# Local attention stage: VectorE picks each head's own block, a projection of 8 matmuls behind the second scores, GpSimd's operands in halves

## The reference, cut to what matters

```python
def _L0_attn_ref(x, W_qkv, W_proj, b_proj, temperature):   # x: tokens, 64 channels, 8 heads of 8
    qkv = (x @ W_qkv.T).reshape(Bb, Nn, 3, NUM_HEADS, HEAD_DIM)
    ...
    attn = jnp.einsum('bhqd,bhkd->bhqk', q, k) * (scale * temperature[0])
    attn = jnp.where(mask[None, None, :, :], attn, -jnp.inf)   # |row|, |column| distance at most 3
    attn = jax.nn.softmax(attn, axis=-1)
    out = jnp.einsum('bhqk,bhkd->bhqd', attn, v)
    out = jnp.transpose(out, (0, 2, 1, 3)).reshape(Bb, Nn, C)
    return out @ W_proj.T + b_proj

h = h + _L0_attn_ref(_layernorm(h, axis=-1), ...)
```

## Time and profile before

| | us |
|---|---|
| median of 3 runs | 1732.75 |
| lowest, highest | 1726.42, 1734.28 |
| the profiled execution | 1732.1 |
| its span from first to last instruction | 1730.3 |
| TensorE busy (matmul) | 1609.0 |
| VectorE busy | 1154.8 |
| ScalarE busy | 1022.5 |
| GpSimd busy | 539.3 |

### The profile page before, as it was taken

The page is one execution under the profiler, slowest core; times in us unless marked ns, Lnnn a source line. Parts: engine busy times, 40 slices in busy tenths (PEclk is TensorE's granted clock), DMA queues, the critical chain, the costliest instruction groups (busy, mean ns, idle before and its releaser), DMA issues.

```text
span 1730.3 us, 88083 instructions
## 1 busy us (share of the span) xinstructions
PE 1609.0 (93%) x32618; PEld 1214.6 (70%) x32618; DVE 1154.8 (67%) x3381; ACT 1022.5 (59%) x2021; POOL 539.3 (31%) x699
## 2 busy tenths in 40 slices
PE   6999999779999999999996899999999999999997
PEld 4677777557888888888874666766676676667663
DVE  2566666545666666666654777787787778777762
ACT  2455555334444444444432477888888788888866
POOL 3311111055555555555542221222222122222210
PEclk9999999869999999999997899999999999999998
DMA  4201101033444444444430233333333333333322
GB/s 113 71 26 29 30 24 30 12 105 108 119 118 119 119 118 118 118 117 118 117 103 24 55 84 83 83 83 88 83 84 87 84 83 83 88 83 84 87 74 58
DMA packets 134691, 143.29 MB, mean 83 GB/s; under 512 B 42498, under 2 KB 90114, under 8 KB 134370
## 3 DMA queue, kind: packets, MB, share of 16 engines
q1 hardware_dynamic: 126306, 116.16, 25.8%
q10 hardware_dynamic: 8320, 26.22, 5.3%
HBM read 66.51 MB, written 16.99 MB: 48 GB/s over the span
## 4 chain that ended last, share of the span: by engine, by line
PE 81%; DVE 5%; issue 5%; SPq 4%; ACT 2%; DMA 1%; POOL 1%; DVEq 0%; ACTq 0%; POOLq 0%
PE ps_D L888 11%; PE ps_D L799 8%; PE ps_OT L818 4%; PE ps_J L838 4%; DVE prob L1436 4%; PE ps_D L676 3%; PE ps_AV L824 3%; SPq L463 3%; PE ps_AV L905 3%; PE ps_D L795 3%; PE ps_J L760 2%; PE ps_OT L752 2%; PE ps_J L996 2%; PE ps_J L964 2%; PE ps_OT L642 2%
## 5 line engine op out<-in xcount | busy, mean ns | idle before, releaser
L1188 ACT ACTIVATE prob<-ps_D 128x1024 bf16<-128x1024 f32 x448 | 460.3, 1031 | 123.1 <-PE ps_D L888 121.4
L1158 ACT ACTIVATE prob<-ps_D 100x512 f32<-100x512 f32 x256 | 139.0, 595 | 220.6 <-PE ps_D L799 220.6
L1351 DVE TENSOR_REDUCE m_sb<-ps_D 128x4 f32<-128x400 f32 x256 | 135.3, 570 | 89.3 <-PE ps_D L776 89.2
L799 PE MATMUL ps_D<-tile_a,key_patch 64*100 64x128 f32 x2048 | 173.8, 288 | 0.2 <-issue 0.2
L888 PE MATMUL ps_D<-tile_a,w_parts 128*128 128x256 bf16 x1024 | 155.6, 279 | 9.2 <-ACT prob L1188 1.9
L888 PE MATMUL ps_D<-tile_b,w_parts 128*128 128x256 bf16 x1024 | 151.1, 272 | 13.7 <-DVE xg L1473 4.3
L799 PEld LDWEIGHTS ps_D<-tile_a,key_patch 64*100 64x100 f32 x2048 | 135.8, 165 | 0.5 <-issue 0.4
L553 POOL TENSOR_TENSOR tile_a<-q_st,q_mask 128x1024 f32<-128x1024 f32 x64 | 123.3, 1927 | 23.0 <-PE ps_D L799 10.5
L795 PE MATMUL ps_D<-mT,key_rows 64*100 64x128 bf16 x1024 | 121.2, 227 | 8.0 <-issue 7.3
L528 POOL TENSOR_TENSOR rstd_bin<-veps_bin,minus_half 128x2 f32<-128x2 f32 x64 | 44.1, 689 | 269.9 <-DVE veps_bin L1249 269.9
L528 POOL TENSOR_TENSOR rstd_ret<-veps_ret,minus_half 128x2 f32<-128x2 f32 x64 | 46.5, 727 | 252.8 <-DVE veps_ret L1249 252.8
(11 more groups left out here) (176 smaller groups left out, 3983.2 us busy)
## 6 DMA issues: line engine op xcount, KB each, us to landing
tile_a<-xg SPq DMA_DIRECT2D x384, 64.0 KB, 2.0
tile_b<-xg SPq DMA_DIRECT2D x384, 64.0 KB, 2.0
key_st<-k_d SPq DMA_DIRECT2D x128, 162.0 KB, 3.1
tile_b<-v_d ACTq DMA_DIRECT2D x128, 120.0 KB
tile_b<-v_d ACTq DMA_DIRECT2D x64, 160.0 KB
w_exp<-experts SPq DMA_DIRECT2D x64, 129.0 KB, 2.3
xT<-in_x SPq DMA_DIRECT2D x32, 256.0 KB, 2.6
k_d<-kpad SPq DMA_DIRECT2D x64, 64.0 KB, 2.8
```

The costliest lines, as they stand in the source:

```text
L799: mm = pe.matmul(s_loc[x][0:NKL, u * P:(u + 1) * P], key_patch[rows_of(x), par, at * NKL:(at + 1) * NKL], q_block[rows_of(x), par, at * P: ...
L1158: act.activation(prob1[0:NKL, 2 * g + x, :], s_loc[x][0:NKL, :], ACT.Exp).then_inc(T2["exp_done"], 1)
L1188: act.activation(sgn[:, k % 4, :], unit(k, par)[:, :], ACT.Sign).then_inc(BN["sign"], 1)
L1351: dve.tensor_reduce(m_sb[:, C * x + HOT[x] + 4 * g:C * x + HOT[x] + 4 * g + 4], m_loc[x][:, 0:4 * NKL].rearrange("p (u n) -> p u n", u=4), ...
```

## The change

`values` signals when the sums of a strip are complete (new semaphore `sums`). `weigh` takes the reciprocal as soon as that signal has come. It then builds the one 128 x 128 block that is needed: one product and three fused product-and-add instructions, each reading one column block of ps_AV and a new 0/1 table `head_mask` (one column for each of the four lane groups), each waiting for the one before it; and a last product with the reciprocals. `project` then needs 8 matmuls with plain weights, and moves behind `scores(i, 1)`. `pre_values` moves up with that and also waits for the reciprocal of the strip before. VectorE does `pre_moments` ahead of `residual`. GpSimd makes query block and key patches of a strip in two halves of four patches each, the first half ahead of `pre_std` and released by the first scores, the second behind it; `peak` waits for its own half. SP's waits count the halves.

```diff
@@ SP, keys_in
-                sp.wait_ge(T2["q_block"], times(i - 1))
+                sp.wait_ge(T2["q_block"], times((i - 1) * 2))
...
-                sp.wait_ge(T2["k_patch"], times((i - 1) * 2))
+                sp.wait_ge(T2["k_patch"], times((i - 1) * 4))
@@ GpSimd, strip_patches(i, pair, par, part)
-                gp.wait_ge(T2["scores"], credited((i - 1) * 2))
+                gp.wait_ge(T2["scores"], credited((i - 1) * 2 - 1 + part))
-                ... q_block of 8 patches, near and far keys of 8 patches
+                ... the same of patches 4 * part to 4 * part + 3
@@ GpSimd, strip
+                if nxt:
+                    strip_patches(i + 2, j + 1, par, 0)
                 if not isinstance(m, int) or m < NS:
                     pre_std(m)
                 if nxt:
-                    strip_patches(i + 2, j + 1, par)
+                    strip_patches(i + 2, j + 1, par, 1)
@@ TensorE, peak(j, par, g)
+                pe.wait_ge(T2["q_block"], times(i * 2 + g + 1))
+                pe.wait_ge(T2["k_patch"], times(i * 4 + 2 * g + 2))
                 if g == 0:
-                    pe.wait_ge(T2["q_block"], times(i + 1))
-                    pe.wait_ge(T2["k_patch"], times((i + 1) * 2))
@@ TensorE, values: behind the sums
+                if g:
+                    mm.then_inc(T2["sums"], 1)
@@ TensorE, project
                 for t in range(2):
-                    for a4 in range(4):
-                        for r in (2 * t, 2 * t + 1):
-                            for x in range(2):
-                                at = C * (r % 2) + 32 * x
-                                mm = pe.matmul(bank["J1"][at:at + 32, t * C:(t + 1) * C], aT1[rows_of(x), a4 * P + 32 * r:a4 * P + 32 * (r + 1)],
-                                               w_p2[rows_of(x), a4, :], start=a4 == 0, stop=a4 == 3)
+                    for r in (2 * t, 2 * t + 1):
+                        for x in range(2):
+                            at = C * (r % 2) + 32 * x
+                            mm = pe.matmul(bank["J1"][at:at + 32, t * C:(t + 1) * C], aT1[rows_of(x), 32 * r:32 * (r + 1)], w_p2[rows_of(x), :], start=True, stop=True)
@@ TensorE, strip
                     pre_turn(m)
+                if m is not None:
+                    pe.wait_ge(T2["rec_done"], times(i))
+                    pre_values(m, 1 - par)
+                scores(j, par, 1)
                 if not first:
                     project(i - 1, min(i + LEAD, NS) if isinstance(i, int) else i + LEAD)
-                if m is not None:
-                    pre_values(m, 1 - par)
-                scores(j, par, 1)
@@ VectorE, weigh
+                dve.wait_ge(T2["sums"], times(i + 1))
+                dve.reciprocal(rec2[:, :], bank["OT"][:, 0:P]).then_inc(T2["rec_done"], 1)
                 dve.wait_ge(T2["av_done"], credited((i + 1) * 2))
-                dve.reciprocal(rec2[:, :], bank["OT"][:, 0:P]).then_inc(T2["rec_done"], 1)
+                dve.wait_ge(T2["proj"], times(i))
+                settle(dve)
+                for hd in range(4):
+                    src, own = bank["AV"][:, hd * P:(hd + 1) * P], head_mask[:, hd:hd + 1]
+                    if hd == 0:
+                        dve.tensor_scalar(aT1[:, 0:P], src, own, None, ALU.mult).then_inc(T2["picked"], 1)
+                    else:
+                        dve.wait_ge(T2["picked"], times(i * 4 + hd))
+                        settle(dve)
+                        dve.scalar_tensor_tensor(out=aT1[:, 0:P], in0=src, scalar=own, in1=aT1[:, 0:P], op0=ALU.mult, op1=ALU.add).then_inc(T2["picked"], 1)
                 dve.wait_ge(T2["rec_done"], times(i + 1))
-                ... one product of 128 x 512 into aT1
+                dve.wait_ge(T2["picked"], times(i * 4 + 4))
+                settle(dve)
+                dve.tensor_tensor(aT1[:, 0:P], aT1[:, 0:P], rec2[:, :], ALU.mult).then_inc(T2["attn_out"], 1)
@@ VectorE, strip
+                if more:
+                    pre_moments(nxt)
                 if not first:
                     residual(i - 1)
-                if more:
-                    pre_moments(nxt)
@@ constants: w_p2 is 128 x 64 instead of 128 x 256, head_mask (128 x 4) is one more transfer in the list of later weights
```

More of the change, by code:

```diff
@@ L80, in shape_tables @@
     t["ones_h"] = np.broadcast_to(np.arange(4)[:, None] == np.arange(32)[None, :] // HD, (P, 4, 32)).astype(np.float32)
+    t["head_mask"] = ((row % 32 // HD)[:, None] == np.arange(4)[None, :]).astype(np.float32)
     keys = np.zeros((2, C, 8, KS, KS), np.float32)
@@ L236, in build @@
         T2 = named("loc", "q_in0", "q_in1", "k_in0", "k_in1", "edge_in0", "edge_in1", "v_in0", "v_in1", "q_block", "k_patch", "max_ps", "max_done", "maxT", "negmax",
-                   "scores", "exp_done", "av_done", "rec_done", "attn_out", "proj", "h_done")
+                   "scores", "exp_done", "sums", "av_done", "rec_done", "picked", "attn_out", "proj", "h_done")
         L = named("pre", "stats", "mv", "veps", "rstd", "minus_mean", "shift", "xn", "xT_ps", "xT_sb", "kq_ps", "v_ps", "k_sb", "q_sb", "v_sb", "stored0", "stored1",
@@ L518, in _, with patches @@
             gp.wait_ge(s_prep, NLAY)
-            def patches(buf):
+            def patches(buf, part):
                 v = buf
-                near = bass.AP(v.tensor, v.offset + 8, [list(v.ap[0]), [1, 8], [NC, QP * KS]])
-                far = bass.AP(v.tensor, v.offset + 9, [list(v.ap[0]), [1, 8], [NC - 2, 2], [W, KS], [NC, 3]])
+                near = bass.AP(v.tensor, v.offset + 8 + 4 * part, [list(v.ap[0]), [1, 4], [NC, QP * KS]])
+                far = bass.AP(v.tensor, v.offset + 9 + 4 * part, [list(v.ap[0]), [1, 4], [NC - 2, 2], [W, KS], [NC, 3]])
                 return near, far
@@ L547, in bias_rows, with strip_patches @@
                                  bias2[:, :].rearrange("p (a c) -> p a c", a=1).broadcast_to((P, 2, C)), ALU.add).then_inc(L["biased"], 1)
-            def strip_patches(i, pair, par):
+            def strip_patches(i, pair, par, part):
+                own = slice(4 * part, 4 * (part + 1))
                 gp.wait_ge(T2["q_in%d" % par], times((pair + 1) * 16))
-                gp.wait_ge(T2["scores"], credited((i - 1) * 2))
+                gp.wait_ge(T2["scores"], credited((i - 1) * 2 - 1 + part))
                 settle(gp)
-                gp.tensor_tensor(q_block[:, par, :].rearrange("c (p h q) -> c p h q", h=NH, q=NQ),
-                                 q_st[:, par, :].rearrange("c (p a q) -> c p a q", a=1, q=NQ).broadcast_to((P, 8, NH, NQ)),
-                                 q_mask[:, :].rearrange("c (a h e) -> c a h e", a=1, e=1).broadcast_to((P, 8, NH, NQ)),
+                gp.tensor_tensor(q_block[:, par, :].rearrange("c (p h q) -> c p h q", h=NH, q=NQ)[:, own, :, :],
+                                 q_st[:, par, :].rearrange("c (p a q) -> c p a q", a=1, q=NQ)[:, own, :, :].broadcast_to((P, 4, NH, NQ)),
+                                 q_mask[:, :].rearrange("c (a h e) -> c a h e", a=1, e=1).broadcast_to((P, 4, NH, NQ)),
                                  ALU.mult).then_inc(T2["q_block"], 1)
@@ L558, in strip_patches @@
                 settle(gp)
-                keys = key_patch[:, par, :].rearrange("c (p n) -> c p n", p=8)
-                near, far = patches(key_st[:, par, :])
+                keys = key_patch[:, par, :].rearrange("c (p n) -> c p n", p=8)[:, own, :]
+                near, far = patches(key_st[:, par, :], part)
                 gp.tensor_copy(keys[:, :, 0:QP * KS], near).then_inc(T2["k_patch"], 1)
@@ L567, in front @@
                 gp.wait_ge(T1["scores"], times(NT))
-                strip_patches(0, 0, 0)
-                strip_patches(1, 0, 1)
+                for i in range(2):
+                    strip_patches(i, 0, i, 0)
+                    strip_patches(i, 0, i, 1)
             def strip(j, par):
@@ L817, in values @@
                             at = prob1[0:NKL, 2 * g + x, :].rearrange("k (p h r c) -> k h p r c", p=4, h=NH, r=QP)[:, 4 * e + hd, :, :, :]
-                            pe.matmul(sums[m, 4 * g:4 * g + 4, :, :], ones_h[0:NKL, hd, :], at, start=hd == 0, stop=hd == 3)
+                            mm = pe.matmul(sums[m, 4 * g:4 * g + 4, :, :], ones_h[0:NKL, hd, :], at, start=hd == 0, stop=hd == 3)
+                if g:
+                    mm.then_inc(T2["sums"], 1)
                 for u in range(4):
@@ L1502, in _ @@
             staggered(dve, strips)
-NFIRST, NLATER, NFIRST_CONST = 12, 32, 7
+NFIRST, NLATER, NFIRST_CONST = 12, 33, 7
 NSTRIP = TOK // 256
@@ L1536 @@
     arr["w_kq2"], arr["w_v2"] = np.concatenate([w[C:2 * C], w[:C]]).T, w[2 * C:].T
-    part = (np.arange(C) // HD % 4)[:, None, None] == np.arange(4)[None, :, None]
-    arr["w_p2"] = np.tile(np.where(part, n(L0_attn_W_proj).T[:, None, :], np.float32(0.0)), (2, 1, 1))
+    arr["w_p2"] = np.tile(n(L0_attn_W_proj).T, (2, 1))
     arr["b_p2"] = n(L0_attn_b_proj).reshape(1, C)
```

9 lines of the change are left out of this document (3 added, 6 removed).

## The result

| | before | changed |
|---|---|---|
| median | 1730.15 us (9 runs, 1726.42 to 1734.28) | 1738.09 us (9 runs, 1736.25 to 1740.17) |
| profiled execution | 1732.1 us, span 1730.3 | 1738.55 us, span 1736.7 |

The ratio of the times is 1.0038, 95% interval 1.0025 to 1.0051. The forecast was 1732.5 us, with a range of 1723 to 1744.

What follows compares the result with a forecast made beforehand. The prediction took TensorE's waiting for ScalarE's copy, not its work, as the limit: loop +2.5 us and stage ends -2.3 us gave +0.2 us on the profiled 1732.1. It forecast 1732.5 us, a tie, range 1723 to 1744.

Steps and rivals of the forecast that it cites:

- The hole: Ahead of pre_values, waiting for ScalarE's copy xnp: removing the projection there gains 0.06 us with par 0, TensorE idles nearly 1 us.
- rival 1: TensorE's work is the bound, as its busy share says: -45 - 12 us, 1675 us; chance 0.08.
- The stall of par 1: First peak with par 1 waits 0.43 us for GpSimd's last key copy; this goes, and pre_values loads 0.51 us earlier.
- the halves' cover: GpSimd's first half, released by earlier scores, is ready early; without that, the 0.43 us stall stays, 12 us in all.
- The projection's new place: Behind the second scores nothing hides the projection: +0.33 us a strip, from 0.26 to 0.53.
- rival 3: The projection behind the second scores reopens a 0.20 us seam: 0.53 us each, +14 us, 1744 us; chance 0.2.
- The ends: Local stage's start and written-out strips: 1.2 us gained at the turn, 0.9 us of stalls; together -2.3 us, 0 to -4.
- GpSimd: Query half 0.96 to 1.2 us, key halves 0.43 and 0.57; at most 0.8 us more a strip, costed at nothing.
- VectorE: Block's products take 1.64 us (1.0 to 2.0), block ready some 0.5 us later than before; costs nothing.
- signs written down as right: Profile after: strip period within 0.1 us of 8.58, VectorE's block finished before the next strip's copy, among others.
- Rival 2: Gap ahead of each loop turn's first scores closes, if instruction issue lags: -8 us, 1724 us; chance 0.13.
- Rival 4: VectorE's last product waits for GpSimd's query half, up to 1.1 us: +18 us, 1750 us; chance 0.06.

Runs made afterwards that it cites:

- The early copy: Changed kernel with the turn of xn ahead of the first scores and ScalarE's copy xnp ahead of the first exponentials: 1714.08 us, ratio 0.9906.
- the run with GpSimd whole: Changed kernel with GpSimd's query block and key patches whole again, behind pre_std: 1739.51 us, ratio 1.0045.
- the run with the waits moved: Changed kernel with the projection's four waits and its settle ahead of the second scores, the projection itself still behind them: 1735.18 us, ratio 1.0025.
- the run with the old place: Changed kernel with the projection of 8 matmuls back between pre_turn and pre_values: 1737.72 us, ratio 1.0045.
- the lagged version: The early copy, plus the projection of strip i - 2 behind the first peak, aT1 holding two blocks by parity: 1693.14 us, ratio 0.9787.

## Why the forecast was a tie and the time was not

**The hole: right.** 44.8 us of waits for xnp in 51 strips of the window, 0.88 us each against 0.8 to 0.9; load 0.11 us behind the copy against 0.12. The early copy, with no work taken away, gave 23 us by the ratios; rival 1, TensorE's work as the bound (1675 us), is out by 63 us.

**The stall of par 1: right in its size,** -0.51 us by the step, and what is left of the strip fits to 0.01 us. Its credit to the halves is wrong: in the run with GpSimd whole the time is the same. What ends the 0.51 us is the copy (709.98), and the projection's leaving the space ahead of pre_values is what makes them. A peak that starts late now only eats into the hole, as the 0.16 us of the run with GpSimd whole do. So the forecast that without the halves' cover 0.43 us would stay, 12 us in all, counted a stall that the hole hides; for the full 0.43 us this is an estimate, from the 1.08 us for which the loads stand idle ahead of pre_values there (at 710.93), and was not run.

**The projection's new place: the step that failed, in its size.** "I take 0.33, the row's own split" should have been 0.46. The load-to-load time was right (0.35). The step looked at the seam behind the projection and left the one ahead of it, whose 0.20 us stood in the row, to the range and to rival 3. The tell I had written down (projection to second peak, over 0.5 us) would have missed it, since it measures between loads; the stretch from scores to sums shows it. Rival 3 had the right place and the right threshold (0.45 us a strip); its price, 0.53, lacks the 0.10 us that the sums come closer to the peak. Its reason, a seam of 0.1 to 0.2 us at every switch to another shape, passed over the one switch that mattered: from the scores to the peak there was none, the load ran ahead, and the projection was put just there. The 0.13 us too little are 7.3 us over 56 strips: with them the sum is +7.5 us in place of +0.2, against +6.4 between the profiled executions and +7.9 between the medians. The loop's part of it is well founded: 28 pairs at +0.34 are 9.5 us, the mended step gives 9.8. That the whole sum comes as close is luck in part, as the next paragraph shows. (The sum gives 1732.3 on the profiled execution and 1732.95 on the medians; the 1732.5 forecast is neither, and the difference changes nothing.)

**The ends: half right.** The start: the turn of the maxima comes 6.62 us after the first peak was asked for (the fifth pre_keys), before 8.04: -1.4, where -1.2 was counted. The written-out strips did not gain the 0.9 us of stalls, nor anything else. From the first scores to the last residual the stage grew by 11.4 us, of which 28 pairs of the loop are 9.5; the eight strips lost 1.9. Stalls like that of the earlier trace rows do not follow the count of matmuls. In the last six strips those of 0.25 us and more, inside a run of like matmuls, add up to 4.2 us before and 6.5 after (the longest 1.28, 1.24, 1.46 and 1.71), but to 2.1 us in the run with the waits moved, whose work is the same. So the ends made +0.5 us (-1.4 and +1.9), where -2.3 was forecast. The rest of the span is 3.6 us shorter besides; 2.5 of that is stage one ending earlier. That varies more between executions: the local stage's first turn, behind a stage one that is the same code in all, comes between 337.99 and 345.58 us in the eleven profiles. This part of the agreement is chance.

**GpSimd: right.** Query half 1.055 us (0.96 to 1.2), key halves 0.46 and 0.62 on the mean (0.43, 0.57), hidden.

**VectorE: right that it is off the path, wrong in when the block is ready.** The products depend on each other. The groups of the changed kernel:

```profile
L1374 DVE SCALAR_TENSOR_TENSOR aT<-ps_AV,head_mask,aT 128x128 f32<-128x128 f32 x162 | 56.8, 351 | 24.2 <-DVE aT L1374 7.1 <-DVE aT L1370 2.5
L1378 DVE TENSOR_TENSOR aT<-aT,rec 128x128 f32<-128x128 f32 x54 | 27.1, 503 | 7.9
```

351 ns each as forecast, but 0.50 us from start to start, with 0.15 us of waiting for the one before. Block ready at 702.19, 1.69 us behind the first peak's load; 0.5 us late was forecast, 1.3 to 1.4 it is. Behind the second scores this costs nothing, in the old place it is what makes the old place no better (the run with eight matmuls there). Two of the signs written down as right did not come: the period of a strip grew by 0.17 us, not by less than 0.1, and with par 1 the block is ready 0.39 us behind the copy (711.21, 710.82), not ahead of it.

**Rival 2** (the gap at the loop's end closes): no, 0.40 us of idleness as before, 6.6 us in the window. **Rival 4** (VectorE and GpSimd collide): the collision is there, and free in the changed kernel; see below.

**What stays open.** Why TensorE loads the peak's weights ahead of time behind the scores, and the projection's not. It is not the semaphore waits, and not the number of matmuls (2, 16 and 64 records show the same 1.36 us). Tile shape, data type and the operands' places were not varied by themselves. Open too is what the picking is worth once the copy comes early: no run has the 32 matmuls in the old place with the early copy. As an estimate they would load for 1.03 us where the eight take 0.35 (700.71 to 701.06), in a place where 0.41 to 0.51 us was idle, so the picking should pay there.

## What to carry to other kernels

Time freed on the busiest engine is worth only what its next piece can start earlier: find, in the timeline, the reader behind the freed piece and the end of what it reads, before counting matmuls. When a piece is moved, measure the stretch between fixed pieces on both sides of its new place; the first and the last load of the piece itself leave both seams out. A hole that is owed to another engine's order is best filled by work whose inputs are a whole turn old, and best shortened by putting the small copy ahead of the long exponentials in that engine's list: here the two together turned +0.4% into -2.1%, and a second small copy moved ahead on ScalarE made it -2.5%.

## What the runs showed of the hardware

**A VectorE product ends with the GpSimd instruction it meets.** The last product of the block, 128 x 128 with both inputs in SBUF, takes 0.29 us where GpSimd stands still (707.11 in the run with the old place, 0.01 us after the query half ended). Beside GpSimd's query half it takes 0.47 us and ends 0.14 us behind that (702.19, the half at 702.05); beside a key copy, with par 1, 0.53 us, again to 0.14 us behind it (711.21, the copy at 711.07). In the lagged version, where it starts early:

```profile
700.62 1.06 POOL L556 TENSOR_TENSOR tile_a<-q_st,q_mask 128x512 f32<-128x512 f32 x1 [1.23 <-PE ps_D L805]
...
700.92 0.90 DVE L1381 TENSOR_TENSOR aT<-aT,rec 128x128 f32<-128x128 f32 x1
```

0.90 us, to 701.82, 0.14 us behind the half's end at 701.68. It waited it out. By the Trainium skill, page "SBUF — State Buffer", section "Who interferes with whom", a VectorE instruction with two SBUF inputs and a GpSimd instruction that reads SBUF exclude each other for the whole instruction; these rows agree, for the order in which GpSimd comes first. The price is bounded by the GpSimd instruction's length, here up to 0.65 us.

In the changed kernel none of it is on the path, since the block is not asked for until the second scores are done. In the lagged version it is. The view of the chain that ended last, in the strip after that one, goes from the product to the maxima, the residual, the moments, GpSimd's root and shift, xn, mT and the turn that TensorE waits for (a piece is counted from where it became the last):

```profile
708.95 0.07 DVE aT L1381
...
709.81 0.12 DVE m_sb L1360
...
712.01 0.71 POOL rstd_pre L530
...
714.41 0.17 ACT mT L1133
...
714.81 0.38 PE ps_T L750 x2
```

The product took 0.94 us there. A collision that was free became part of the next limit as soon as ScalarE's hole was closed. What it costs was not measured; as an estimate, at most the 0.4 us a strip for which the turn waits.

**A seam has a place.** Between the second scores and the peak the next weights are loaded 0.11 us ahead of their first matmul. Behind the peak they are not, whatever comes (the sums 704.24, pre_values 706.59 in the run with the early copy, the projection 700.71 in the lagged one: load and first matmul start together). So the same eight matmuls cost 0.46 us where they break a pair of pieces that overlap, and 0.35 us from load to load where nothing is lost.
